# Gated layer in split fp16: low-rank product in one pass of two parts, down product in three passes of parted operands

## The reference

```
def _qlinear(x, q, scale, A, Bm):
    w = (q.astype(jnp.float32) - Q_ZERO) * (scale * Q_STEP)[:, None]
    y = jnp.einsum('bsh,oh->bso', x, w)
    return y + LR_SCALE * (x @ A @ Bm)
g = _qlinear(x, gate_q, gate_scale, gate_A, gate_B)
u = _qlinear(x, up_q, up_scale, up_A, up_B)
h = jax.nn.silu(g) * u
return _qlinear(h, down_q, down_scale, down_A, down_B)
```

## Time and profile before

| | us |
|---|---|
| median of 3 runs | 1540.02 (1538.23 to 1542.85) |
| span of the profiled execution | 1535.8 |
| first stage, until the first instruction of the second | 0 to 112.6 |
| gated stage, until PE's last down product | 112.6 to 513.5 |
| PE busy | 1354.5 (88% of the span) |
| DVE busy | 1031.6 (67%) |
| ACT busy | 835.2 (54%) |
| mean granted TensorE clock | 0.942 |

### The profile page before, as it was taken

How to read it: one execution, slowest core, us unless ns; L and a number is a source line. 1 busy time by engine, 2 the same in 40 slices (tenths; PEclk the granted TensorE clock), 3 DMA queues, 4 the chain that set the end, 5 groups by cost and what they waited for, 6 DMA issues and landing times. The chain is left out here.

```text
span 1535.8 us, 35207 instructions
## 1 busy us (share of the span) xinstructions
PE 1354.5 (88%) x10502; PEld 719.6 (47%) x10598; DVE 1031.6 (67%) x3495; ACT 835.2 (54%) x1550; POOL 464.0 (30%) x1396
## 2 busy tenths in 40 slices
PE   8948999999999699389989899898989989986996
PEld 4413444444444355245545455455545545543563
DVE  5884545545453289588878788787878878861553
ACT  2613423314031167367768677676767768773553
POOL 3650000000000233233433343333433433331664
PEclk9976999999999899779999999999999999998997
DMA  9300000000000045701000111001111000002221
GB/s 338 131 12 30 1 1 0 0 0 0 0 0 0 4 128 159 223 28 38 17 28 35 39 38 38 11 34 35 38 39 38 26 18 35 13 8 49 62 70 48
DMA packets 65106, 69.52 MB, mean 45 GB/s; under 512 B 35214, under 2 KB 53774, under 8 KB 64300
## 3 DMA queue, kind: packets, MB, share of 16 engines
q1 hardware_dynamic: 64940, 67.38, 13.4%
HBM read 36.96 MB, written 19.92 MB: 37 GB/s over the span
## 5 line engine op out<-in xcount | busy, mean ns | idle before, releaser
L1321 DVE TENSOR_REDUCE arena<-bank 128x32 f32<-128x512 f32 (+3 forms) x768 | 395.6, 550 | 111.0 <-PE bank L1168 55.7
L1259 ACT ACTIVATE arena<-bank 128x512 f32<-128x512 f32 x576 | 337.0, 613 | 177.6 <-PE bank L1179 103.4
L1165 PE MATMUL bank<-arena 96*128 96x512 bf16 (+3 forms) x768 | 249.4, 349 | 27.0 <-issue 19.3
L1179 PE MATMUL bank<-arena 123*128 123x512 bf16 x576 | 225.5, 397 | 10.2 <-ACT arena L1259 7.1
L1198 PE MATMUL bank<-arena 128*32 128x128 f32 x4608 | 171.0, 276 | 12.6 <-ACT arena L1259 12.4
L577 PE MATMUL bank<-arena 128*128 128x512 f16 (+1 forms) x704 | 168.0, 381 | 0.0
L1417 POOL TENSOR_SCALAR arena<-arena 128x128 bf16<-128x128 bf16 x384 | 142.6, 371 | 46.9 <-DVE arena L1367 22.9
L586 PE MATMUL bank<-arena 128*128 128x512 f32 (+1 forms) x352 | 152.7, 593 | 1.6 <-DVE arena L710 1.6
L649 ACT ACTIVATE arena<-bank 128x512 f32<-128x512 f32 (+1 forms) x88 | 52.5, 596 | 173.8 <-PE bank L574 173.7
L1405 POOL TENSOR_TENSOR arena<-arena 128x4 f32<-128x4 f32 x128 | 25.4, 199 | 378.1 <-DVEq L1339 378.0
L1198 PEld LDWEIGHTS bank<-arena 128*32 128x32 f32 x4608 | 119.4, 109 | 43.0 <-ACT arena L1259 24.6
(11 more groups left out here) (186 smaller groups left out, 2207.9 us busy)
## 6 DMA issues: line engine op xcount, KB each, us to landing
arena<-qk_rows SPq DMA_DIRECT2D x16, 960.0 KB, 5.0
qk_rows<-arena SPq DMA_DIRECT2D x16, 768.0 KB, 4.1
arena<-arena SPq DMA_DIRECT2D x32, 256.0 KB, 2.9
arena<-in_x SPq DMA_DIRECT2D x4, 1024.0 KB, 12.3
out<-arena SPq DMA_DIRECT2D x16, 256.0 KB, 2.2
qk_rows<-arena SPq DMA_DIRECT2D x16, 192.0 KB, 4.6
arena<-in_down_qT SPq DMA_DIRECT2D x1, 2816.0 KB, 25.8
arena<-in_up_qT SPq DMA_DIRECT2D x1, 2752.0 KB, 18.0
```

What stands on the lines that cost most here:

```text
L1165: last = pe.matmul(bank[:, 0:k1 - k0], query_aug[st.slot][0:ROWS, h * P:(h + 1) * P], key_aug[st.p][0:ROWS, k0:k1], start=True, stop=not d ...
L1179: last = pe.matmul(bank[:, :], key_aug[st.p][0:KROWS, j * P:(j + 1) * P], query_aug[st.slot][0:KROWS, f * N:(f + 1) * N], start=True, stop ...
L1259: act.activation(probs[u % PROBS], back_bank[u % 2][:, :], ACT.Exp, scale=float(HD) ** -0.5).then_inc(probs_ready, 1)
L1321: dve.tensor_reduce(out=cm[:, h * 64 + k0 // CHUNK:h * 64 + k1 // CHUNK], in_=score_bank[bank_of_score(front, number)][:, 0:k1 - k0].rearr ...
```

## The change

Line numbers with a plus are those of the changed kernel. Four things are changed.

1. **Low-rank product.** The factor B and t = x @ A are each cut into two fp16 parts where they had three bf16 parts. They are laid out in the 96 rows so that one fp16 matmul (new L575) sums what two bf16 matmuls did. `cut_factor` has three steps in place of four, with fewer and smaller operations; `t_parts` has two operations for each of gate and up, in place of four.
2. **Down product.** h and the down weights are each kept as an fp16 high part and an fp16 rest, and each fp32 matmul becomes three fp16 matmuls: high by high, high by rest, rest by high (new L591).
3. **Parting.** For this, DVE's h goes to a buffer of its own, ACT copies it to fp16 (`keep_h`, new L651), and DVE subtracts that from h (`part_h`, new L718). The down weights get the same at the stage's head: an ACT copy (new L678) and a DVE subtraction (new L767) for each of the 11 blocks.
4. **Scales.** h is kept 16 times larger than before (the factor `H_UNIT`, put into the scales), with one more small DVE multiplication; 512 words more of work space.

The core of the diff:

```diff
-                first, second = low[k]
-                cols = slice(i * P, i * P + r)
-                pe.matmul(m.banks[2 + k][0:r, :], first[:, cols], t_first[k][0:TRIPLE, :], start=True, stop=False)
-                pe.matmul(m.banks[2 + k][0:r, :], second[:, cols], t_second[k][0:TRIPLE, :], start=False, stop=True).then_inc(low_made, 1)
+                pe.matmul(m.banks[2 + k][0:r, :], low[k][:, i * P:i * P + r], t_parted[k][0:TRIPLE, :],
+                          start=True, stop=True).then_inc(low_made, 1)
...
-                    last = pe.matmul(m.banks[6 + t % 2][:, :], m.f32(HT_AT + i * D + t * P, P)[0:r, :],
-                                     m.f32(WD_AT + i * D, D)[0:r, :], start=i == 0, stop=i == IT - 1)
+                    h_high, h_rest = halves_of(HT_AT, i)
+                    w_high, w_rest = halves_of(WD_AT, i)
+                    for n, (left, right) in enumerate(((h_high, w_high), (h_high, w_rest), (h_rest, w_high))):
+                        last = pe.matmul(m.banks[6 + t % 2][:, :], left[0:r, t * P:(t + 1) * P], right[0:r, :],
+                                         start=i == 0 and n == 0, stop=i == IT - 1 and n == 2)
...
-                pe.wait_ge(h_ready, g * IT + (IT + 1))
+                pe.wait_ge(h_high_ready, g * IT + (IT + 1))
+                pe.wait_ge(h_rest_ready, g * IT + (IT + 2))
...
+            def keep_h(g, i):
+                r = rows(i)
+                act.wait_ge(h_ready, g * IT + (i + 2))
+                act.activation(halves_of(HT_AT, i)[0][0:r, :], h[i % 2][0:r, :], ACT.Copy).then_inc(h_high_ready, 1)
...
+                        if k == 0 and i > 0:
+                            keep_h(g, i - 1)
...
+                keep_h(g, IT - 1)
                 if not last_group:
                     for t in range(G):
                         keep(g + 1, t)
...
+            for i in range(IT):
+                act.wait_ge(wd_summed, i + 1)
+                act.activation(halves_of(WD_AT, i)[0][0:rows(i), :], wd[i % 2][0:rows(i), :], ACT.Copy).then_inc(wd_high_ready, 1)
             act.wait_ge(rstd_ready, 1)
             for t in range(G):
                 normed(0, t)
...
-                    seq.mark(dve.tensor_copy(t_first[k][0:TRIPLE, :], t_all[k][0:TRIPLE, :]))
+                    seq.mark(dve.tensor_copy(t_parted[k][0:TRIPLE, :], t_all[k][0:TRIPLE, :]))
                     seq.wait(dve)
-                    seq.mark(dve.tensor_tensor(out=t_rest[k][0:TRIPLE, :], in0=t_all[k][0:TRIPLE, :], in1=t_first[k][0:TRIPLE, :], op=ALU.subtract))
-                    seq.wait(dve)
-                    seq.mark(dve.tensor_copy(t_second[k][0:TRIPLE, :], t_rest[k][0:TRIPLE, :]))
-                    seq.wait(dve)
-                    dve.tensor_tensor(out=t_second[k][last, :], in0=t_rest[k][last, :], in1=t_second[k][last, :],
+                    dve.tensor_tensor(out=t_parted[k][last, :], in0=t_all[k][last, :], in1=t_parted[k][last, :],
                                       op=ALU.subtract).then_inc(t_ready, 1)
...
+            def part_h(g, i):
+
+                r = rows(i)
+                high, rest = halves_of(HT_AT, i)
+                dve.wait_ge(h_high_ready, g * IT + (i + 2))
+                dve.tensor_tensor(out=rest[0:r, :], in0=h[i % 2][0:r, :], in1=high[0:r, :], op=ALU.subtract).then_inc(h_rest_ready, 1)
...
+                    if i > 0:
+                        part_h(g, i - 1)
+                part_h(g, IT - 1)
```

And `cut_factor` on POOL, whose step 3 is gone:

```diff
                 if step == 0:
-                    alone(pool.tensor_copy(second, B))
-                    alone(pool.tensor_copy(first[one, :], B[one, :]))
+                    alone(pool.tensor_copy(factor, B))
                 elif step == 1:
-                    alone(pool.tensor_tensor(out=rest, in0=B, in1=second, op=ALU.subtract))
+                    alone(pool.tensor_tensor(out=rest[two, :], in0=B[two, :], in1=factor[two, :], op=ALU.subtract))
                 elif step == 2:
-                    alone(pool.tensor_copy(first[two, :], rest[two, :]))
-                    alone(pool.tensor_copy(first[three, :], rest[three, :]))
-                elif step == 3:
-                    alone(pool.tensor_copy(second[two, :], rest[two, :]))
-                    alone(pool.tensor_tensor(out=first[three, :], in0=rest[three, :], in1=first[three, :], op=ALU.subtract))
+                    alone(pool.tensor_copy(factor[two, :], rest[two, :]))
```

## The result

| | before | changed |
|---|---|---|
| median | 1539.86 (1538.23 to 1542.85) | 1495.8 (1492.17 to 1496.19) |
| ratio | | 0.9709, 95% interval 0.9694 to 0.9725 |
| span of the profiled execution | 1535.8 | 1490.4 |
| first stage | 112.6 | 106.1 |
| gated stage, from its first matmul's start to that of its last one | 400.2 | 361.3 |

The account below looks back on a forecast made before the run. PE was taken as the bound in the gated stage, DVE in the first stage. The terms -37.1 - 17.8 + 6.5 + 1.9 - 7.1 + 4.6 = -49.0 us took 1540.0 to 1491 us, range 1482 to 1503.

Parts of the forecast that it names:

- down product: Gated stage: 33 fp16 matmuls for 11 fp32 ones, 7.16 us a tile in place of 9.48, 16 tiles; 37.1 us less.
- low-rank product: Gated stage: 88 half steps of nine matmuls in place of ten, with longer waits behind groups; 17.8 us less.
- parting inside the half steps: Half steps: ACT's copy and DVE's subtraction of h fit beside PE's work; nothing, with 0.7 us to spare.
- ends of groups: Ahead of the down product: parting of h is bare, 1.7 us three times and 1.4 in the last group; 6.5 more.
- head: Start of the gated stage: `low_t` 3.1 us later, shorter `t_parts` gives 1.2 back; 1.9 us more.
- first stage: Fewer POOL operations in `cut_factor` take DVE stalls with them; 7.1 us less.
- clock: Gated stage: two falls of PE's granted clock taken for six new waits; 4.6 us more, range none to 13.8.
- two operations fewer ahead of the first half step: Head of the gated stage: `t_parts` loses a 0.69 us operation and a cast taken as 0.49; 1.2 us back.
- `low_t` runs at the lower clock: Head of the gated stage: possible extra of up to 3.65 us, on top of the 1.9.
- The later start: Head of the gated stage: normalisations behind the last weight copy start `low_t` at about 139.0, not 135.92; 3.1 us later.
- two falls at 2.3: Gated stage, new waits at and behind groups' ends: two clock falls of 2.3 us lost each; 4.6 us more.
- all six new waits swing the clock: Rival, waits at and behind groups' ends: 9.2 us above the forecast, with slow `low_t` 3.65 more, 1504; chance 0.08.

Follow-up runs that it names:

- e3: Changed kernel without the parting of h: h in one fp16 part, the third pass multiplies the high part again; 1484.03 us.
- e4: Changed kernel with DVE's subtraction of each block issued twice, the first time into unused memory; 1499.94 us.
- e1: Kernel before with the low-rank part of the change alone, keeping the fp32 down product; 1513.83 us.
- e2: Changed kernel with the low-rank part put back, so the down product's change alone; 1520.76 us.
- e12: Changed kernel with a fourth pass in the down product, rest of h times rest of the weights; 1529.34 us.
- e9: Changed kernel with PE waiting for the last blocks' parts at their own matmuls, and ACT keeping two turned tiles before parting the last block; 1482.65 us.
- e8: Changed kernel with POOL's removed step 3 of `cut_factor` put back as work into unused memory; 1499.63 us.
- e5: Changed kernel run once more, unaltered; 1495.12 us.
- e10: Changed kernel with the first group's four normalisations placed between the copies of the down weights instead of behind all eleven; 1489.55 us.
- e11: Changed kernel with the late wait, the early normalisations and the early first gate combine together; 1470.92 us.
- e6: Changed kernel with ten unused fp16 matmuls on PE behind the last down product of groups 1 to 3; 1490.3 us.
- e7: Changed kernel with DVE combining the next group's first gate block ahead of the last tile's residual sum; 1487.67 us.

## Why the prediction was right, and where it was not

The forecast was 1491 us, measured 1495.8, inside the range. By its own steps, in spans:

| step | predicted | measured |
|---|---|---|
| down product | -37.1 | 16 x (7.13 - 9.48) = -37.6 |
| low-rank product | -17.8 | 88 x 0.217 less, waits 1.3 more: -17.8 |
| parting inside the half steps | 0 | 0 (e3, e4) |
| ends of groups | +6.5 | 3 x 1.67 + 1.42 = +6.4 |
| head | +1.9 | 36.27 - 31.18 = +5.1 |
| first stage | -7.1 | -6.5 (-7.5 on DVE) |
| clock | +4.6 | 3 x 1.7, 0.6 less behind the head: +4.5 |
| sum | -49.0 | -45.9; the spans differ by 45.4 |

**Right, and shown by runs that add or take the part:** the low-rank product (e1), the down product (e2 and e12), the cover of the parting (e3 and e4), the ends (e3 and e9) and the first stage (e8). The first stage's 7.1 lies between the 6.5 of this profile and the 7.6 of e5's.

**The step that failed is the head.** The prediction wrote of `t_parts`: "two operations fewer ahead of the first half step, L690's 0.69 and a cast [...]: 1.2 us back." PE waited for DVE's parts before, and I took them off without asking what came second. It was ACT's six copies out of bank 0 (3.59 us behind `low_t`), which the first half step overwrites: PE's wait went from 4.22 to 3.96, and of 1.2 us 0.26 came back. e1 shows it without any parting of weights. That it is these copies stands in the trace, as the releaser, and in PE's list; no run moves the wait. And "if `low_t` runs at the lower clock, up to 3.65 us on top" was left out of the sum: it took 5.74 us, 2.1 more, and in all ten profiled executions with the new head order 5.05 to 6.64. Whether that order causes it is not settled: e1 and e10, whose turns run through as before, show 5.48 and 5.32, and only before and e11 the 3.65 of full clock, though e11 has e10's head order. The later start was well sized, 3.1 against 3.26. So the head cost 0.2 + 2.1 + 0.9 = 3.2 us more than the sum had. The other steps make that 3.1 for all spans (-45.9 against -49.0); what else the median missed, 1.7 us, is less than the later stages vary with the same instructions, and less than the 3.6 us between this profiled execution and the median.

**The clock** came out at the right sum from wrong terms, by luck: two falls at 2.3 were taken, and there were three at 1.7, less 0.6 behind the head; with e5's five it would have been 7.9. The Trainium skill's section "A second HAM failure mode: psum-queue depth-cycling" (page "TensorE: Matmul & The Clock Gate"), would, as the prediction read it, have had all six new waits swing the clock; three of six did in the first profile and five in e5's. Over all profiles it was 31 of 54 such waits (table below), between that reading and "none", so a forecast can only give a share.

## What to carry to other kernels

When a chain of operations is made shorter, look for what is ready second: the gain ends there, and a bank that is still being read counts like data that is missing. A wait for all of a buffer in front of a loop costs as much as its last piece is late; put it in front of the matmul that reads that piece (8.1 us here, more than the 6.4 that the change lost by it). Splitting an fp32 matmul into fp16 parts pays only by the products left out: four passes cost what fp32 costs, three a quarter less.

## What the runs showed of the hardware

**The clock falls at short waits, and not at the same ones.** Counted over the profiled executions, in the gated stage behind its head:

| PE's wait | falls |
|---|---|
| behind a group's last tile, 1.46 to 2.27 us, fp32 down tiles (before, e1) | 0 of 6 |
| the same, fp16 down tiles (changed, e2 to e5, e8 to e10, e12) | 17 of 27 |
| 2.01 us between two pairs of turned tiles (changed, e2, e4 to e8, e10, e12) | 14 of 27 |
| 3.05 to 4.07 us ahead of the last down product (the same nine) | 4 of 9 |
| 0.3 us behind a group, the rest of the wait filled with matmuls (e6) | 0 of 3 |
| 0.34 us between the turned tiles (before, e1, e3, e9, e11) | 0 of 15 |
| 0.59 to 1.03 us behind a group (e7, e11) | 0 of 6 |
| 1.63 us ahead of the last down product (before, e1, e3) | 0 of 3 |

One kernel run twice (changed and e5) has three falls and five. e1 and e3 have the same waits behind a group (2.27, 2.24 and 1.89 us), behind fp32 tiles in e1 with no fall, behind fp16 tiles in e3 with two; but e12, with fp16 tiles and these waits, has none there either. What decides between two waits of the same length stays open. Each fall costs about 1.7 us.

**DVE's short operations stall most.** Opposite a POOL subtraction of 3 us an operation on one element per row (L213) took 2.77 us in place of 0.15, as long as one on 512 (L219, 2.90).
